# The second batch of a last mixture-of-experts layer, routed as the first is

## What is computed

```python
x = x + attn0(layernorm(x))   # 16 heads of 16: short convolution, delta rule
x = x + ffn0(layernorm(x))    # 8 experts, top 2, and a shared expert
x = x + attn1(layernorm(x))   # 16 heads of 128, 2 kv heads, causal, softcap 30
x = x + ffn1(layernorm(x))    # 16 experts, top 6
# ffn1, h the normed tokens (the auxiliary loss is not returned):
scores = softmax(h @ gate_w.T);  topk_w, topk_idx = top_k(scores, 6)
cw = zeros(T, 16).at[arange(T)[:, None], topk_idx].add(topk_w)
for e in range(16):
    y += cw[:, e:e+1] * ((silu(h @ w_gate[e].T) * (h @ w_up[e].T)) @ w_down[e].T)
```

## Time and profile before

| what | us |
|---|---|
| median of 3 runs (847.88 to 848.25) | 848.23 |
| the profiled execution | 845.31 |
| its span, first to last instruction | 843.5 |

### The profile page before, as it was taken

The page is one execution under the profiler, slowest core; times in us unless marked ns, Lnnn a source line. Parts: engine busy times, 40 slices in busy tenths (PEclk is TensorE's granted clock), DMA queues, the critical chain, the costliest instruction groups (busy, mean ns, idle before and its releaser), DMA issues.

```text
span 843.5 us, 14393 instructions
## 1 busy us (share of the span) xinstructions
PE 792.2 (94%) x4825; PEld 548.0 (65%) x4825; DVE 482.7 (57%) x1166; ACT 361.2 (43%) x756; POOL 218.0 (26%) x318
## 2 busy tenths in 40 slices
PE   5998799879989998899999999989999999999998
PEld 3576566666657786677777767766765545455557
DVE  5999866766522226866565565757745373324443
ACT  3988777646113324352232342323256676211111
POOL 3644654111610034111112111116712233200000
PEclk9988999999989999999999999999999999999999
DMA  4001780082253322033542322212333423293431
GB/s 143 2 1 28 225 299 2 2 222 85 89 162 102 100 69 63 26 103 121 140 135 68 101 67 68 75 38 91 111 80 113 137 88 121 68 291 128 125 126 50
DMA packets 95807, 85.72 MB, mean 102 GB/s; under 512 B 34792, under 2 KB 84456, under 8 KB 95736
## 3 DMA queue, kind: packets, MB, share of 16 engines
q1 hardware_dynamic: 88200, 70.05, 28.3%
q0 software_dynamic: 4224, 11.74, 4.0%
q10 hardware_dynamic: 3312, 3.02, 1.1%
HBM read 57.02 MB, written 26.71 MB: 99 GB/s over the span
## 4 chain that ended last, share of the span: by engine, by line
PE 73%; DVE 11%; ACT 6%; issue 6%; POOL 2%; DMA 2%; SPq 0%; ACTq 0%; DVEq 0%; POOLq 0%
PE bank L1488 9%; PE bank L1451 7%; PE bank L1345 6%; PE bank L1306 6%; PE bank L1331 6%; PE bank L1267 5%; PE bank L1283 5%; PE bank L730 4%; PE bank L756 3%; PE bank L953 3%; PE bank L2309 3%; PE bank L975 2%; PE bank L2266 2%; PE bank L2293 2%; POOL rows_in L1205 2%
## 5 line engine op out<-in xcount | busy, mean ns | idle before, releaser
L1607 ACT ACTIVATE arena<-bank 128x512 f32<-128x512 f32 (+1 forms) x96 | 46.9, 525 | 148.5 <-PE bank L1451 148.5
L1229 POOL TENSOR_TENSOR arena<-arena,causal_t 128x256 f32<-128x256 f32 x64 | 45.1, 726 | 218.1 <-ACT arena L1612 218.0
L1488 PEld LDWEIGHTS bank<-arena 128*128 128x128 f32 x640 | 76.2, 191 | 4.3 <-POOL arena L1229 2.9
L1488 PE MATMUL bank<-arena 128*128 128x129 f32 x640 | 77.1, 275 | 1.7 <-POOL arena L1229 1.7
L1451 PE MATMUL bank<-arena 128*128 128x512 f32 (+3 forms) x256 | 76.2, 442 | 1.4 <-DVE arena L1685 1.4
L1540 ACT ACTIVATE arena<-bank 128x512 f32<-128x512 f32 (+1 forms) x39 | 20.2, 521 | 118.1 <-PE bank L1267 108.3
L1306 PE MATMUL bank<-arena 128*128 128x256 f32 (+1 forms) x272 | 67.9, 389 | 2.5 <-DVE arena L1665 2.4
L1267 PE MATMUL bank<-xnT,arena 128*128 128x512 f32 (+1 forms) x168 | 65.8, 514 | 0.5 <-issue 0.5
L1306 PEld LDWEIGHTS bank<-arena 128*128 128x128 f32 (+1 forms) x272 | 52.0, 194 | 21.2 <-issue 10.7
L1345 PE MATMUL bank<-arena 128*128 128x256 f32 x256 | 61.0, 381 | 2.7 <-DVE arena L1692 2.0
L1345 PEld LDWEIGHTS bank<-arena 128*128 128x128 f32 x256 | 48.1, 190 | 23.6 <-issue 12.8
(11 more groups left out here) (296 smaller groups left out, 1491.6 us busy)
## 6 DMA issues: line engine op xcount, KB each, us to landing
arena<-in_w_gu SPq DMA_DIRECT2D x44, 256.0 KB, 3.7
rows_in<-place SPq DMA_DIRECT2D x5, 1664.0 KB, 14.6
arena<-in_w_dn SPq DMA_DIRECT2D x34, 128.0 KB, 3.5
rows<-arena SPq DMA_DIRECT2D x8, 544.0 KB, 4.6
arena<-in_w_dn SPq DMA_DIRECT2D x24, 176.0 KB
arena<-in_wq SPq DMA_DIRECT2D x32, 128.0 KB, 3.1
arena<-in_wo SPq DMA_DIRECT2D x32, 128.0 KB, 2.0
arena<-rows SPq DMA_DIRECT2D x32, 128.0 KB, 2.1
```

Source lines behind the costliest of these rows:

```text
L1229: nc.gpsimd.tensor_tensor(blocks, blocks, causal_t[:].unsqueeze(1).to_broadcast([P, 2, P]), ALU.mult).then_inc(s_p, 1)
L1488: mm = nc.tensor.matmul(b_o[pair][:, t * (DH + 1):(t + 1) * (DH + 1)], pr[:, o:o + P], v[:, grp, kt, :], start=(kt == 0), stop=(kt == qb))
L1607: nc.scalar.activation(th[:, sbank * 512:sbank * 512 + w], b_s[sbank][:, 0:w], ACT.Tanh, scale=SCALE / SOFTCAP).then_inc(s_th, 1)
```

## The change

The dense half is removed, with its weight loads, the combine weights in DRAM and their broadcast. Batch 1 goes through the same path as batch 0, and the loops over passes run over 64 (`2 * NP1`) instead of 32.

- Norm and ranking of batch 1 are pulled forward: statistics at step 3, the two square roots together at step 3 on ACT, transposes at step 5, gate logits at step 6, ranking at 6 to 11, `places1(1)` at 12 (behind gate and up of pass 13), `rows1_read` and the new `rows1_base` (the first half of `rows1_index`) at 12, the rest at 13 to 20. The last head's transposes move from step 1 to 0 and its projection from 2 to 1.
- POOL scatters batch 1's 24 sets of rows ahead of `send_back(13)`, in four lots of six, each lot waiting for the one before. The ring `py` has 18 buffers instead of 10.
- The ring `xr` has five buffers instead of four. SP writes zeros into a second `rows1` in eight more DMAs of 544 KB during attention, and issues the load-back of batch 0 between `load_rows(51)` and `load_rows(52)`. DVE adds batch 0 back at steps 51 to 62.
- At the end SP and ACT issue three load-backs each for batch 1. DVE adds two of its four token tiles. For the other two PE sums over k, `sum_back`, with twelve matmuls against the diagonal matrices `dg`, which DVE makes at steps 40 to 45 (`spread_weights`), and DVE adds that sum in one residual.

```diff
...
-    xr = at(37900, NX * DIM).rearrange("p (r n) -> p r n", r=NX)
+    xa = [at(o, 4 * XW).rearrange("p (t d) -> p t d", t=4) for o in (36812, 14600)]
+    xr = at(37900, NW * DIM).rearrange("p (r n) -> p r n", r=NW)
...
-    NY = 10
-    py = [at(8192 + DIM * i, DIM) for i in range(NY)]
+    NY = 18
+    py = [at(8192 + DIM * i, DIM) for i in range(16)] + [at(20000 + DIM * i, DIM) for i in range(2)]
...
-    ys = [at(o, 4 * DIM).rearrange("p (t d) -> p t d", t=4) for o in range(0, K1 * 4 * DIM, 4 * DIM)]
+    ys = [at(o, 4 * DIM).rearrange("p (t d) -> p t d", t=4) for o in (16912, 17936, 18960, 22048, 12288, 13312)]
+    dg = at(14600, 2 * K1 * P).rearrange("p (i n) -> p i n", n=P)
...
-            if r == 2:
-                step(dve, nc.vector.tensor_scalar(c.mk, c.lg[:], float(K), None, ALU.is_lt))
-                nc.vector.tensor_reduce(c.mks, c.mk.rearrange("p t e -> p e t"), AX.X, ALU.add).then_inc(s_pl, 1)
-                return
-            nc.vector.scalar_tensor_tensor(out=c.cw[:, :, 0:E], in0=c.lg[:], scalar=float(K), in1=c.ex[:],
-                                           op0=ALU.is_lt, op1=ALU.mult).then_inc(s_cw, 1)
...
+            step(dve, nc.vector.tensor_scalar(c.mk, c.lg[:], float(K), None, ALU.is_lt))
+            nc.vector.tensor_reduce(c.mks, c.mk.rearrange("p t e -> p e t"), AX.X, ALU.add).then_inc(s_pl, 1)
 
         def places1(self, pe, h):
             c, bk = scr[2 + h], p_pos[h]
             pe.wait_ge(s_pl, MK1[h])
+            if h:
+                pe.wait_ge(s_oT, 2 * NH)
...
+        def spread_weights(self, dve, k):
+            if k == 0:
+                dve.wait_ge(s_rows, SC + 2 * SC1)
+            for t in (2, 3):
+                ins = nc.vector.scalar_tensor_tensor(out=dg[:, 2 * k + t - 2, :], in0=ident[:], scalar=wk1[:, 1, k, t:t + 1],
+                                                     in1=ident[:], op0=ALU.mult, op1=ALU.mult)
+            if k == K1 - 1:
+                ins.then_inc(s_rx1, 1)
+
+        def sum_back(self, pe):
+            pe.wait_ge(s_rx1, 3)
+            for k in range(K1):
+                pe.wait_ge(s_ys[k], ys_0[k] + 32)
+                for t in (2, 3):
+                    mm = nc.tensor.matmul(b_y[0][:, (t - 2) * DIM:(t - 1) * DIM], dg[:, 2 * k + t - 2, :], ys[k][:, t, :],
+                                          start=(k == 0 and t == 2), stop=(k == K1 - 1), skip_group_check=True)
+            mm.then_inc(s_y, 1)
+
         def add_back(self, dve, h, i):
             k, t = i // 4, i % 4
             n = 4 * h + t
-            dve.wait_ge(s_ext, EX0 + 16 + 16 * K1)
+            dve.wait_ge(s_ys[k], ys_0[k] + 16 * (h + 1))
...
-            if J >= NX:
-                sp.wait_ge(s_px, NB + J - NX + 1)
-            sp.dma_start(xr[:, J % NX, :], rows1[h][j * P:(j + 1) * P, 0:DIM]).then_inc(s_xl[J % NX], 16)
-
...
+            if J >= NW:
+                sp.wait_ge(s_px, NB + J - NW + 1)
+            sp.dma_start(xr[:, J % NW, :], rows1[h][j * P:(j + 1) * P, 0:DIM]).then_inc(s_xl[J % NW], 16)
+
+        def load_back(self, eng, h, ks):
+            eng.wait_ge(s_ret, RE0 + 16 * (h + 1) * NP1)
+            for k in ks:
+                eng.dma_start(ys[k], ret[h][1 + k * HALF:1 + (k + 1) * HALF, :].rearrange("(t p) d -> p t d", p=P)).then_inc(s_ys[k], 16)
...
-                if 2 <= n < 10:
-                    q = n - 2
-                    sp.dma_start(rows1[0].rearrange("(a p) d -> p a d", p=P)[:, 4 * q:4 * q + 4, :],
+                if 2 <= n < 18:
+                    h, q = (n - 2) // 8, (n - 2) % 8
+                    sp.dma_start(rows1[h].rearrange("(a p) d -> p a d", p=P)[:, 4 * q:4 * q + 4, :],
                                  zr.unsqueeze(1).to_broadcast([P, 4, XW])).then_inc(s_zf, 16)
-            for J in range(NP1):
+            for J in range(2 * NP1):
                 self.load_rows(sp, J)
-                if J == 1:
+                if J in (1, NP1 + 1):
+                    h = J // NP1
                     sp.wait_ge(s_qr, len(order))
...
+                    sp.dma_start(ext[h], rows1[h].rearrange("(j p) d -> p j d", p=P)[:, :, DIM:XW]).then_inc(s_ext, 16)
+                if J == NP1 + 19:
+                    self.load_back(sp, 0, range(K1))
+            sp.wait_ge(s_xres.sem, 16)
+            sp.dma_start(io["out"][:, 0:4, :], x_sb[:, 0:4, :]).then_inc(s_out, 16)
+            self.load_back(sp, 1, range(0, K1, 2))
             for q in range(2):
-                sp.wait_ge(s_xres.sem, 17 + q)
+                sp.wait_ge(s_xres.sem, 18 + q)
...
-            for J in range(NP1):
+            for J in range(2 * NP1):
+                if J == R0:
+                    for t in range(4):
+                        self.send_rows(pool, 1, t * K1, (t + 1) * K1)
                 self.send_back(pool, J)
...
-            for J in range(NP1):
-                if J + 2 < NP1:
+            for J in range(2 * NP1):
+                if J + 2 < 2 * NP1:
                     self.pair_turn(pe, J + 2)
-                if J:
+                if J == 0:
+                    self.turn(pe, NH - 1)
+                else:
                     self.pair_hidden(pe, J - 1)
                 if J == 1:
-                    self.turn(pe, NH - 1)
-                if J == 2:
                     self.project(pe, NH - 1)
-                if J == 9:
+                if J == 5:
                     self.ln_turn(pe, 10)
-                if J == 10:
                     self.ln_turn(pe, 11)
-                if J == 12:
+                if J == 6:
                     pe.wait_ge(ln_xT, 4 + 12)
                     self.logits(pe, 3)
-                if J == 22:
-                    self.cw_turn(pe)
-                if J + 1 < NP1:
+                if J + 1 < 2 * NP1:
                     self.pair_gate_up(pe, J + 1, offs[J + 1])
-                if J + 3 < NP1:
+                if J + 3 < 2 * NP1:
                     offs.append(owners(J + 3))
+                if J == 12:
+                    self.places1(pe, 1)
                 if J:
                     self.pair_down(pe, J - 1, offs[J - 1])
...
+            self.pair_hidden(pe, 2 * NP1 - 1)
+            self.pair_down(pe, 2 * NP1 - 1, offs[2 * NP1 - 1])
+            self.sum_back(pe)
...
-            for J in range(NP1):
-                if J + 2 < NP1:
+            for J in range(2 * NP1):
+                if J + 2 < 2 * NP1:
                     self.pair_copy_gu(act, J + 2)
                     self.pair_x(act, J + 2)
-                if J + 1 < NP1:
+                if J == 5:
+                    self.ln_evac(act, 10)
+                    self.ln_evac(act, 11)
+                if J + 1 < 2 * NP1:
                     self.pair_silu(act, J + 1)
                 if J:
                     self.pair_y(act, J - 1)
-                if J == 5:
+                if J == 3:
                     self.ln_std(act, 10)
+                    self.ln_std(act, 11)
                 if J == 6:
-                    self.ln_std(act, 11)
-                if J == 9:
-                    self.ln_evac(act, 10)
-                if J == 10:
-                    self.ln_evac(act, 11)
-                if J == 13:
                     self.exps(act, 3)
-                if J == 22:
-                    self.cw_evac(act)
...
+            self.pair_y(act, 2 * NP1 - 1)
+            act.wait_ge(s_xres.sem, 16)
+            self.load_back(act, 1, range(1, K1, 2))
...
-            for J in range(NP1):
+            for J in range(2 * NP1):
                 if J:
                     self.pair_h(dve, J - 1)
-                if J == 1:
+                if J == 0:
                     self.turned(dve, NH - 1)
                 self.pair_mul(dve, J)
                 self.pair_copy_dn(dve, J)
-                if J == 0:
-                    self.rows1_mine(dve, 0)
-                if J == 1:
-                    self.rows1_slot(dve, 0)
+                if J in (0, NP1 + 3):
+                    self.rows1_mine(dve, J // NP1)
+                if J in (1, NP1 + 4):
+                    self.rows1_slot(dve, J // NP1)
+                if J in (2, NP1 + 5):
+                    self.rows1_back(dve, J // NP1)
                 if J == 2:
-                    self.rows1_back(dve, 0)
-                if J == 3:
                     dve.wait_ge(s_y, NH)
                     self.residual(dve, 4, b_y[0])
                     self.residual(dve, 6, b_y[1])
+                if J == 3:
+                    self.ln_stats(dve, 10)
+                    self.ln_stats(dve, 11)
                 if J == 4:
-                    self.ln_stats(dve, 10)
-                if J == 5:
-                    self.ln_stats(dve, 11)
+                    self.ln_norm(dve, 10)
+                    self.ln_norm(dve, 11)
+                if J == 6:
+                    self.route_a(dve, 3)
                 if J == 7:
-                    self.ln_norm(dve, 10)
+                    self.route_soft(dve, 3)
+                    self.route_over(dve, 3)
                 if J == 8:
```

(37 more changed lines are left out.)

## The result

The kernel after takes 867.64 us (median of 4, 866.95 to 870.08), the kernel before 848.24: a ratio of 1.0234, 95% interval 1.0213 to 1.0255. It is slower by 2.3%, where 841.0 was forecast, 26.6 too low. The profiled execution's span is 865.2 us; 836.3 was forecast for it, so 28.9 are to be explained there. (The profiled execution of the kernel before was 2.9 under its median, that of the kernel after 0.7; this is the difference between 26.6 and 28.9.)

What follows compares the result with a forecast made beforehand. PE was taken as the bound. Its passes, with +0.3 us of corrections, end at 816.2; a 20.1 us tail gives a span of 836.3, 7.2 under 843.5, so the median is 848.23 - 7.2 = 841.0 us, range 837 to 848.

Steps and rivals of the forecast that it cites:

- The scatters on POOL, which are moved ahead of `send_back(13)`: POOL from step 13: four lots take 36.3 us, landed at 713.9; rows 3.7 us to spare, no stall; send-backs catch up.
- the end of the last passes: Steps 62 and 63 take 4.58 us like today's 30 and 31; exposed last hidden and down take 2.03.
- the tail: From PE's end of passes to the span's end: last send, loads, sums, residual and output, 20.1 us (bounds 16.5 to 24.6).
- What is pulled forward: Batch 1's routing moved beside early passes: five corrections to PE's time, summing to +0.3 us.
- the trip for the square roots: Both roots share one ACT function-table trip, costing 0.9 us instead of 2.3 for two, a gain of 1.35.
- `places1(1)`, base and index: Steps 12 and 13: `places1(1)` adds 1.1 us on PE; DVE's base and index make PE lose 0.25 and 0.65, together 0.9.
- The end: After PE's passes, an exposed DRAM round trip, 20.1 us in all, including 11.3 for six loads.
- the way from the last send to the loads: In the tail: SP starts loading 3.08 us after POOL starts the last send.
- The load-back beside the passes: Batch 0's load-back from step 44 delays `load_rows(52)` by 11.3 us, wanted 16.7 us on: covered.
- Rival 1: POOL's queue becomes the bound: each send takes longer beside DVE's work; at 0.3 us more, 852 us. Chance 0.09.

Runs made afterwards that it cites:

- no_sends_b1: Kernel after without batch 1's 24 row scatters on POOL; SP copies batch 0's sorted rows in eight plain DMAs instead: 842.39 us, ratio to before 0.9938.
- after_paced_all: Kernel after with a 384-element POOL memset before each batch 1 row scatter and send-back from 13 on, looser lot waits, ring `py` of 20: 846.46 us, ratio 0.9957.
- plain_dma_in_lots: Kernel before with 24 extra plain DMAs of SP in lots of six beside the passes, nothing extra on POOL: 850.06 us, ratio 1.0009.
- the lots: Kernel before with 24 extra POOL scatters, six back to back ahead of send_back 4, 11, 18 and 25, each lot awaited: 871.85 us, ratio 1.0275.

## Why the prediction was wrong

The step that failed is "The scatters on POOL, which are moved ahead of `send_back(13)`". It counted POOL's time and who waits for POOL, found 3.7 us to spare, and set the cost to everybody else at nothing. POOL's side came about as counted: the 24 row sends took 0.99 us each on average, and the last started at 713.6, some 2.4 later than counted. The cost is on engines that wait for nothing that POOL makes: PE's steps beside the row sends and the backlog behind them grew by 22.7 us.

The sum, from the first gate and up of pass 0 to that of pass 63: the forecast implies 182.4 (step 62 at 809.6, its gate and up 0.35 on, less 627.55); after took 208.8, `no_sends_b1` 186.1 and `after_paced_all` 182.3. So of the 28.9:

- 26.4 us: steps that grew. Without the row scatters 22.7 of them go. `no_sends_b1` still has three steps with such waits, 4.7 us longer in all: two (2.2 and 1.4) beside the send-backs that leave together when batch 1's indices come, one (1.1) beside four that leave together behind the load-back. With the pauses these go too. The rest of its passes is 1.0 under the forecast.
- 2.0: the first pass starts at 629.56 instead of 627.55. Other profiles have it at 628.8 to 635.5 (632.3 in `plain_dma_in_lots`, which has nothing but one more memset before the passes), so this arises in earlier stages and varies. At 325 us ACT is 0.3 behind the kernel before, at 329 us 1.7; the granted clock from 328 to 332 us is 0.57 for 1.00, behind the wait of 4.52 us above. Nothing of the change stands there, and kernels without it have the same, so most of these 2.0 us aren't its cost.
- 1.0: the end of the last passes, of which 0.9 are the last down at half clock, 1.98 instead of 1.08.
- -0.5: the tail, 19.6 for 20.1.

**What is pulled forward** came out right: in `after_paced_all`, 1.1 us of the 182.3 is rows that came late, so the rest is 1.2 under the forecast. PE waited 0.5 us in the trip for the square roots, set at 0.9; `places1(1)`, base and index lengthened steps 12 and 13 by 1.4 and 0.3, set at 2.0 together. **The end** came out right: the six loads took 11.2 for 11.3, and PE's eight matmuls at half clock 1.99 for 1.9; only the way from the last send to the loads was 0.7 shorter than set. The load-back beside the passes was covered: from 780 us on all steps but one (3.04) took 2.79, until the last.

**Rival 1** had the right place and the wrong mechanism. It looked for a cost of each send on POOL's own clock; sends didn't grow (0.98 on average for the 64 send-backs, had 0.96 to 1.01). The rule weighed there (the Trainium skill, SBUF — State Buffer, Who interferes with whom) isn't what costs the time here: without DVE's fast copy the lots cost the same, 871.3 against 871.9, and with both copies one element wide no less, 876.4. The chance of 0.09 for "slower" was too low for a stretch of which the rival itself said that no trace shows such a backlog.

**What the trace of before could have told.** Its rows of scatters at full rate, all stand beside attention, where this profile shows no late hand-over; beside the passes it never has two sends at 1.27 apart. The forecast took "no harm seen" from one stage and one rate into another, and from a single execution, which shows less harm than the 19 others.

## What to carry to other kernels

A move of indirect DMAs is a change for the engines beside them, not for POOL alone: ask at what spacing they will stand, beside which stage, and whether the trace shows that pair. If waits without a named releaser come up on ACT and DVE while POOL issues scatters, and steps of PE grow with them, try a pause between the scatters before anything else; here some 0.15 us more apart was worth some 20 us. Then spend pauses only where there is a backlog, since each one delays the queue's end.

## What the runs showed of the hardware that was not expected

- Indirect DMAs on POOL at a spacing of 1.27 or 1.43 us held up what PE hands to ACT and DVE beside the passes, with waits of up to 9.6 us; at 1.56 us and more, over 24 in a row, not at all. So the effect goes from nearly whole to nothing between 1.43 and 1.56 (the two kernels differ besides in the length of the memset and in two ring buffers).
- It depends on what PE does: the same lots cost 1.5 us beside the dense half (up to 4.0 with its matmuls split) and 24 beside the passes. Register loads, copies, bytes, landings, signal and matmul rate are each by itself ruled out as the cause; the mechanism isn't known.
- Beside the dense matmuls of the first layer, gathers 1.25 us apart went with a wait of ACT of 4.4 to 4.6 us in 19 profiles and 2.21 in one, and mostly with a lower granted clock behind it. One profile of a kernel doesn't show what its other executions do.
- Plain DMAs that POOL issues, with the same packets and bytes, did no harm.
